# A four-layer graph network on one core: twelve stored pairs in place of ten, slots cleared by ScalarE, codes made behind takes

## What is computed

```python
def _rgcn_conv(x, src, dst, edge_type, edge_weight, W, root, bias):
    xj = x[src]
    m = jnp.zeros((xj.shape[0], W.shape[2]), dtype=x.dtype)
    for r in range(W.shape[0]):
        mask = (edge_type == r).astype(x.dtype)[:, None]
        m = m + mask * (xj @ W[r])
    m = m * edge_weight[:, None]
    out = jax.ops.segment_sum(m, dst, num_segments=x.shape[0])
    return out + x @ root + bias
...
h = jax.nn.relu(_rgcn_conv(x, src, dst, edge_type, ew, W1, root1, b1))
h = _rgcn_conv(h, src, dst, edge_type, ew, W2, root2, b2)
...
x = _layernorm(x + _L3_gnn_ref(...), axis=-1)
```

## Time and profile before

| | |
|---|---|
| median of 3 runs | 3843.97 us (3838.03 to 3846.60) |
| the profiled execution | 3840.92 us, span 3838.9 us |
| mean granted TensorE clock | 0.957 |
| TensorE / VectorE / ScalarE / POOL busy | 3455.1 / 2470.5 / 2042.3 / 2647.7 us |
| first late pass, first to last gather | 1990.6 to 2929.6 us |
| second late pass, first to last gather | 2946.3 to 3826.2 us |

### The profile page before, as it was taken

How to read it: one execution, slowest core, us unless ns; L and a number is a source line. 1 busy time by engine, 2 the same in 40 slices (tenths; PEclk the granted TensorE clock), 3 DMA queues, 4 the chain that set the end, 5 groups by cost and what they waited for, 6 DMA issues and landing times. The chain is left out here.

```text
span 3838.9 us, 70907 instructions
## 1 busy us (share of the span) xinstructions
PE 3455.1 (90%) x23412; PEld 2961.8 (77%) x23412; DVE 2470.5 (64%) x7952; ACT 2042.3 (53%) x4808; POOL 2647.7 (69%) x2736
## 2 busy tenths in 40 slices
PE   6999999999999999699978888888886899999995
PEld 5999888998887888588856666676665778888885
DVE  6999998998976555766666665666562354444431
ACT  4555555555546555556565555555555444544453
POOL 5777777777752666365547777777776777777776
PEclk8999999999999999799989999999997999999997
DMA  7666666666675666466634444444443444444453
GB/s 232 191 190 191 187 190 182 189 193 188 186 214 129 157 160 158 112 161 171 171 102 149 145 151 146 149 149 154 143 154 100 132 142 150 150 141 144 148 157 91
DMA packets 438499, 609.19 MB, mean 159 GB/s; under 512 B 266274, under 2 KB 310818, under 8 KB 437987
## 3 DMA queue, kind: packets, MB, share of 16 engines
q1 hardware_dynamic: 310162, 342.89, 28.6%
q0 software_dynamic: 100624, 234.79, 23.5%
q10 hardware_dynamic: 27330, 26.78, 2.3%
HBM read 451.89 MB, written 152.35 MB: 157 GB/s over the span
## 5 line engine op out<-in xcount | busy, mean ns | idle before, releaser
L660 POOL DMA_INDIRECT work<-table_rel,reli x1454 | 1378.2, 948 | 488.7 <-issue 435.6
L660 POOL DMA_INDIRECT work<-table_pre,srci x831 | 815.5, 981 | 263.2 <-issue 259.6
L2709 ACT ACTIVATE work<-iota,local 128x72 f32<-128x72 f32 x1456 | 376.4, 341 | 456.4 <-PE bank L1715 452.0
L1715 PEld LDWEIGHTS bank<-work 128*128 128x128 f32 x2912 | 392.6, 203 | 231.6 <-DMA work<-table_rel,reli 213.8
L1715 PE MATMUL bank<-work 128*128 128x72 f32 x2912 | 405.6, 285 | 163.6 <-DMA work<-table_rel,reli 162.9
L2714 ACT ACTIVATE work<-work,ew,src_both 128x72 f32<-128x72 f32 x1456 | 512.1, 434 | 6.1
L1416 PE MATMUL bank<-counts,piece_hi 128*128 128x468 f32 x1176 | 462.0, 393 | 17.2 <-issue 9.6
L1044 ACT ACTIVATE X<-bank 128x468 uint8<-128x468 f32 (+1 forms) x624 | 327.8, 544 | 280.9 <-PE bank L986 276.4
L947 PE MATMUL bank<-w_both,work 128*128 128x256 f32 x1664 | 433.7, 386 | 18.3 <-DVE work L881 9.8
L1416 PE MATMUL bank<-counts,piece_lo 128*128 128x468 f32 x1176 | 448.0, 381 | 0.0
L959 PE MATMUL bank<-work 128*128 128x64 f32 x3328 | 400.5, 274 | 3.7 <-DVE hist L828 2.9
(11 more groups left out here) (335 smaller groups left out, 6022.0 us busy)
## 6 DMA issues: line engine op xcount, KB each, us to landing
work<-ea_cols SPq DMA_DIRECT2D x208, 256.0 KB, 2.9
kept<-work SPq DMA_DIRECT2D x50, 720.0 KB
kept<-w_both SPq DMA_DIRECT2D x50, 720.0 KB
work<-kept SPq DMA_DIRECT2D x50, 720.0 KB
w_both<-kept SPq DMA_DIRECT2D x50, 720.0 KB
adj<-X SPq DMA_DIRECT2D x156, 225.0 KB
work<-adj SPq DMA_DIRECT2D x60, 585.0 KB
work<-table_rel,reli POOLq DMA_INDIRECT x1454
```

The source lines that it names most:

```text
L660: pool.indirect_dma_start(into[:, u, :], None, tables[p], bass.IndirectOffsetOnAxis(ap=idx_of(p)[:, t:t + 1].bitcast(U32), axis=0)).then_i ...
L1715: mm = pe.matmul(bank[4 + m % LATE_BANKS][:, 0:PAIR_WIN], late_gat[n % LATE][:, u, :], late_hot[:, n % LATE_HOTS, u * PAIR_WIN:(u + 1) * P ...
L2709: ins = act.activation(hot3[:, u, :], iota[:, 0:PAIR_WIN], ACT.Abs, bias=local[:, t:t + 1], scale=-1.0)
```

## The change

Lines are those of the changed file in the rows of order below, of the file before elsewhere.

- `PERIOD` goes from 10 to 8: twelve stored pairs, 8, 16, ... 96; 120 units in place of 100. Ten units fall on eight turns by `TURN`, so turns 1 and 5 of every eight use two units. Their columns are 37 wide in place of 36. The extra pairs of pass 4 stay six, from 19 on in steps of 16.
- The slot of the first unit of a turn is cleared by ScalarE (`clear_slot`), at the end of step h, for the unit that is used at turn h-1; VectorE waits for it. A second unit of a turn is still cleared by VectorE.
- VectorE makes the codes of unit k+2 behind the takes of unit k, one tile's low parts behind each of four codes (`tile_lo`, `extra_lo`), and loads a half's registers behind the half before.
- In pass 3 TensorE begins a turn that uses two units with the use of the first. In pass 4 the extra unit's use moves from the middle of the turn to a place ahead of the next fill's first half and of the pair's.
- Some small arrays move to other places.

```diff
-PERIOD = 10
+PERIOD = 8
-GW = 36
+GW = 37
-UNIT_AT = {PERIOD * (k // (2 * RANGES)) + k % (2 * RANGES): k for k in range(D_UNITS + 1)}
-BUILD_AT = {h - 1: k for h, k in UNIT_AT.items()}
+TURN = (0, 1, 1, 2, 3, 4, 5, 5, 6, 7)
+TURNS_OF = [PERIOD * (k // len(TURN)) + TURN[k % len(TURN)] for k in range(D_UNITS + 1)]
+USED_AT = {h: [k for k in range(D_UNITS + 1) if TURNS_OF[k] == h] for h in range(-1, PAIRS + 6)}
+CLEARED_AT = {h: ks[0] for h, ks in USED_AT.items() if ks and 2 <= ks[0] < D_UNITS}
-X_EVERY, X_FIRST, X_N = 15, 17, 6
+X_EVERY, X_FIRST, X_N = 16, 19, 6
...
@@ late_dve
-                if p == 3 and BUILD_AT.get(h, D_UNITS) < D_UNITS:
-                    unit_codes(dve, BUILD_AT[h])
-                take_at = BUILD_AT if p == 3 else UNIT_AT
-                if h - 1 in take_at:
-                    unit_take(dve, p, take_at[h - 1])
-                if p == 3 and BUILD_AT.get(h + 1, 1) % RANGES == 0 and BUILD_AT[h + 1] < D_UNITS:
-                    half_lo(dve, BUILD_AT[h + 1] // RANGES)
+                for k in USED_AT.get(h if p == 3 else h - 1, ()):
+                    unit_take(dve, p, k)
...
@@ unit_codes
             ins.then_inc(code_ready, 1)
+            if n % RANGES and n // RANGES + 1 < D_UNITS // RANGES:
+                tile_lo(dve, n // RANGES + 1, n % RANGES - 1)
...
@@ unit_take
                 put_unit(dve, k)
+                if k + 2 < D_UNITS:
+                    unit_codes(dve, k + 2)
+                if (k + 1) % RANGES == 0 and k + 1 < D_UNITS:
+                    d_places[:] = load_within(dve, PAIRS + (k + 1) // RANGES * U + 1)
@@ put_unit
-            if k % RANGES == 0:
-                d_places[:] = load_within(dve, PAIRS + k // RANGES * U + 1)
-            if k >= 2:
-                dve.wait_ge(a_used, USES_BEFORE + k - 1)
-                dve.wait_ge(a_stored[k % 2], KEPT_BEFORE + k // 2 * 16)
-            done(dve, dve.memset(late_a[k % 2][:, :, :, TW:], 0.0))
+            if k in CLEARED_AT.values():
+                dve.wait_ge(high_or_clear, CLEARS_BEFORE + list(CLEARED_AT.values()).index(k) + 1)
+            else:
+                if k >= 2:
+                    dve.wait_ge(a_used, USES_BEFORE + k - 1)
+                    dve.wait_ge(a_stored[k % 2], KEPT_BEFORE + k // 2 * 16)
+                done(dve, dve.memset(late_a[k % 2][:, :, :, TW:], 0.0))
...
@@ late_pe
+                second_half = new[-1] if len(new) > 1 or len(used) > 1 and new else D_UNITS
+                if p == 3 and len(used) > 1:
+                    unit_use(pe, p, used.pop(0))
+                if new:
+                    unit_fill(pe, new[0], 0)
+                if p == 4 and h - 1 in X_AT:
+                    extra_use(pe, X_AT[h - 1])
                 if p == 4 and h in X_AT:
                     extra_fill(pe, X_AT[h], 0)
...
                 node(pe, h)
-                if build < D_UNITS:
-                    unit_fill(pe, build, 2)
-                if p == 4 and h - 1 in X_AT:
-                    extra_use(pe, X_AT[h - 1])
+                if len(used) > 1:
+                    unit_use(pe, p, used.pop(0))
+                if new and new[0] != second_half:
+                    unit_fill(pe, new[0], 2)
+                if len(new) > 1:
+                    unit_use(pe, p, used.pop(0))
+                    unit_fill(pe, new[1], 0)
                 if p == 4 and h in X_AT:
                     extra_fill(pe, X_AT[h], 2)
                 if not built:
                     pair_half(pe, p, h, 1)
-                if unit < D_UNITS:
-                    unit_use(pe, p, unit)
+                if second_half < D_UNITS:
+                    unit_fill(pe, second_half, 2)
+                for k in used:
+                    unit_use(pe, p, k)
...
+        def clear_slot(act, k):
+            act.wait_ge(a_used, USES_BEFORE + k - 1)
+            act.wait_ge(a_stored[k % 2], KEPT_BEFORE + k // 2 * 16)
+            act.activation(late_a[k % 2][:, :, :, TW:], zeros_b[:, 0:GW - TW].unsqueeze(1).unsqueeze(1)
+                           .broadcast_to([P, RHI, RELS, GW - TW]), ACT.Copy).then_inc(high_or_clear, 1)
@@ late_act
                 node(h - LATE_HOTS)
+                if p == 3 and h - 1 in CLEARED_AT:
+                    clear_slot(act, CLEARED_AT[h - 1])
```

More of the change, by code:

```diff
@@ L261, in gnn @@
         d_lo = b2b_row[:, 0:D_COLS]
-        d_w = [b1a_row[:, i * D_COLS:(i + 1) * D_COLS] for i in range(PIECES)]
+        d_w = [b1a_row[:, i * D_COLS:(i + 1) * D_COLS] for i in range(PIECES - 1)]
         d_sum = more[:, 0:2 * GC].rearrange("p (o c) -> p o c", o=2)
@@ L276, in gnn @@
         x_codes, *x_w = (src_hi[:, x_at + i * X_COLS:x_at + (i + 1) * X_COLS] for i in range(1 + PIECES))
-        x_lo = b2b_row[:, D_COLS:D_COLS + X_COLS]
+        x_lo = count[:, D_COLS + X_COLS:D_COLS + 2 * X_COLS]
+        x_end = x_at + (1 + PIECES) * X_COLS
+        d_w.append(src_hi[:, x_end:x_end + D_COLS])
         staging_x = view(11280 + D_COLS, X_COLS).bitcast(I32)
@@ L1461, in late_dve @@
                 built_setup(dve, in_dense, d_tmp, d_first, d_lo, d_code, d_w)
-                half_lo(dve, 0)
+                for u in range(U):
+                    tile_lo(dve, 0, u)
                 dense_setup(dve)
             else:
-                extra_lo(dve, 0)
+                for u in range(U):
+                    extra_lo(dve, 0, u)
             places = {}
             if p == 3:
-                unit_codes(dve, BUILD_AT[-1])
+                d_places[:] = load_within(dve, PAIRS + 1)
+                for n in range(2):
+                    unit_codes(dve, n)
+            else:
+                x_places[:] = load_within(dve, PAIRS + D_COLS + 1)
             for h in range(PAIRS + LATE_LAG):
@@ L1549, in dense_setup, with tile_lo, extra_lo @@
             done(dve, dve.tensor_copy(places[:, :, 0:1], firsts[0:1, :, 0:1]))
[L1551 to L1565, removed]
+        def tile_lo(dve, half, u):
+            at = half * U + u
+            for i in range(PIECES):
+                dve.tensor_scalar(late_lo[:, half % 2, u * PIECES + i, :], iota_b[:, :], d_lo[:, at:at + 1],
+                                  d_w[i][:, at:at + 1], ALU.is_equal, ALU.mult)
+        def extra_lo(dve, half, u):
+            at = half * U + u
+            for i in range(PIECES):
+                dve.tensor_scalar(late_lo[:, half % 2, u * PIECES + i, :], iota_b[:, :], x_lo[:, at:at + 1],
+                                  x_w[i][:, at:at + 1], ALU.is_equal, ALU.mult)
         def unit_codes(dve, n):
@@ L1590, in extra_codes @@
             ins.then_inc(code_ready, 1)
+            if k % RANGES and k // RANGES + 1 < X_UNITS // RANGES:
+                extra_lo(dve, k // RANGES + 1, k % RANGES - 1)
         def extra_take(dve, k):
@@ L1605, in extra_take @@
                 put_tile(dve, x_a, u, x_places).then_inc(x_taken, 1)
+            if (k + 1) % RANGES == 0 and k + 1 < X_UNITS:
+                x_places[:] = load_within(dve, PAIRS + D_COLS + (k + 1) // RANGES * U + 1)
         def extra_sum(dve, k):
@@ L1610, in extra_sum, with uses, builds @@
                 dve.tensor_copy(x_sum[:, k // RANGES % 2, :], bank[X_BANK][:, 0:GC]).then_inc(x_summed, 1)
+        def uses(h):
+            return [k for k in USED_AT.get(h, ()) if k < D_UNITS]
+        def builds(h):
+            return uses(h + 1)
         def takes_before(p, k):
@@ L1662, in late_pe @@
             if p == 3:
-                unit_fill(pe, BUILD_AT[-1], 0)
-                unit_fill(pe, BUILD_AT[-1], 2)
+                unit_fill(pe, 0, 0)
+                unit_fill(pe, 0, 2)
             for h in range(PAIRS):
                 m = (p - 3) * PAIRS + h
-                unit = UNIT_AT.get(h, D_UNITS)
-                build = BUILD_AT.get(h, D_UNITS) if p == 3 else D_UNITS
+                used = uses(h)
+                new = builds(h) if p == 3 else []
                 if p == 3 and h == PAIRS - 1:
@@ L1678, in late_pe @@
                     if h in D_PAIRS:
-                        pe.wait_ge(a_taken, sums_taken(p, unit))
+                        pe.wait_ge(a_taken, sums_taken(p, USED_AT[h][0]))
                     else:
@@ L2013, in low @@
             def low(k):
-                dve.wait_ge(x_high, k + 1)
+                dve.wait_ge(high_or_clear, k + 1)
                 split_low(dve, k, rows[k])
@@ L2310, in pieces_low @@
             if k < CHUNKS:
-                dve.wait_ge(x_high, CHUNKS + k + 1)
+                dve.wait_ge(high_or_clear, CHUNKS + k + 1)
                 split_low(dve, k, X[:, k * CT:(k + 1) * CT, :])
@@ L2460, in late3_sp @@
             for h in range(-1, PAIRS + 4):
-                k = BUILD_AT.get(h, D_UNITS)
-                if k < D_UNITS:
+                for k in builds(h):
                     sp.wait_ge(a_taken, takes_before(3, k) + U)
@@ L2839, in late4_sp @@
             for h in range(PAIRS + 5):
-                if UNIT_AT.get(h, D_UNITS) + 2 < D_UNITS:
-                    load(UNIT_AT[h] + 2)
+                for k in uses(h):
```

(2 more changed lines are left out.)

12 lines of the change are left out of this document (4 added, 8 removed).

## The result

The changed kernel takes **3895.18 us** (median of 4 runs, 3892.89 to 3896.49), the kernel before 3845.28 us beside it; the ratio is 1.0128, 95% interval 1.0115 to 1.0141. It is slower by 50 us. The forecast was 3891.

What follows compares the result with a forecast made beforehand. POOL bounds the kernel before; after the change TensorE bounds the first late pass. First pass +67, second -20: +47 us on the profiled 3840.9, which is 3.1 below the median 3844.0, giving 3891 us; range 3806 to 3930.

Steps and rivals of the forecast that it cites:

- The stops: First late pass: TensorE stands for ScalarE's relu, delayed by the moved clear, 15 x 4.6 + 4 x 3.74 = 84 us.
- The first pass: First late pass, first to last gather: 922 us without waits for the relu, 1006 with them, 67 us longer than before.
- The second pass: Second late pass: POOL stays the bound at 860 us, TensorE needs some 835, so 20 us are gained.
- rival 4: Second late pass does not gain, TensorE at 885 us; +25, 3916 us; chance only within the forecast's 0.62.
- TensorE has become the bound: First late pass: with 862 us of own work TensorE, not POOL, sets the end, by 3 us, before waits for the relu.
- the stops change their cause: First late pass: nothing extra for the clock, since the 880 us before ran at 0.96 granted with 82 waits for gathers.
- 889 + 84 = 973: First late pass: TensorE through 96 turns at 15 + 862 + 12 = 889 us, plus 84 us of waits for the relu.
- rival 2: First late pass: each of 19 waits for the relu also costs some 1.8 us of clock; +34, 3925 us; chance 0.04.
- No wait, no gain: First late pass: codes behind takes cause no wait at the second fill and no gain against 12 us of waits kept.
- Rival 1: First late pass: no new wait at L2400 for the relu, pass ends at 922 us; -37, 3807 us; chance 0.24.

## Why the prediction was right

- **The stops.** I forecast 15 of 4.6 us where the pair is gathered and 4 of 3.7 where it is built, 84 us. Measured in the window: 15 of 4.5 and 4 of 3.65, 82.3 us. ScalarE's clear, priced at 1.06 us between two other sizes, took 1.09. Four experiments (the relu ahead, the clears back on VectorE, the clears alone, ten pairs) make this shown and not only argued.
- **The first pass.** 1006 us from first to last gather forecast, 1013.0 measured; +67 against +74.
- **The second pass.** 860 forecast, 857.8 measured. TensorE's waits for the take, 63.3 us before, are gone from its list, and rival 4 (they stay and take the gain) was tried: it costs 19 us of the kernel's time, 24 of the pass, where I had 25. Its words "240 + 60 products" should be 120 + 60, as in the sum.
- **Two terms were mis-sized against each other, and the sum hid it.** That the two errors nearly cancel was luck. I gave TensorE 862 us for its own work up to turn 96, and so had it as the bound by 3 us even without the stops ("**TensorE has become the bound**"). Between its first gathered matmul and the end of the last unit's product it worked 811.6 us with the relu ahead: 50 less, and it is not the bound there, since POOL ran at its own pace and TensorE waited 27.7 us for gathers. And I put nothing on the clock ("the stops change their cause"). With the stops the same work took 849.5 us, 38 more; from 2010 to 2890 the granted clock was 0.50 for 99 us, with the relu ahead for 37. So the changed kernel was through 965.5 us after the first gather, where the sum has 889 + 84 = 973. Behind turn 96 the sum has 33 us and the trace 47.5, with one more stop at the relu, 6.1 us at 2961.8, that I had not looked for. Why 862 was too much is not settled; it was scaled from a stage that ran at 0.96, which can be part of it.
- **The clock.** Each of the 19 stops has its own stretch at a granted clock of 0.50, 3.4 or 6.8 us long and 106 us in all, and between 2010 and 2960 there is none elsewhere: 0.53 granted over the 5 us behind the stop above, 1.00 on both sides. The earlier trace rows show the same behind one wait of 4.35 us. The 38 us are 2.0 us a stop, so rival 2 is right that the clock is paid on top, and its 1.8 us were about right; its time (3925) came out too long because the own work was 50 us too high. I weighed it against the wrong row, the average clock of the stage before, whose 82 waits for gathers are short, 2.7 us at most; the last section shows that short and long waits of one total are not alike.
- **VectorE's chain.** "No wait, no gain" for codes behind takes holds with ScalarE's clears as far as it was tried, with the relu ahead and POOL as the bound (2 us). It fails once VectorE clears (41 us): the codes then stand ahead of the clear in steps that begin late, and a sum copy that I had not placed in the chain makes some of them late.
- **Rival 1** (no new stop, 3807) did not come, but its time is what the kernel gives when the stop is taken out: 3801.

## What to carry to other kernels

An instruction that waits holds up all that stands behind it in its engine's order (here a clear of 1.09 us, behind whose wait TensorE stood 82.3 us): before moving even a 1 us clear to a half-idle engine, write down what stands behind it there and who needs that next. A stop on an engine that is not the bound cost nothing here and showed nothing in the time (83.1 us of stops, 3841.87 us against 3841.30), so a part that measured as harmless may cost all of its stops when a later part uses up the slack; test parts together with the one that moves the bound. When work is cut into a chain of producers, place every instruction of the consumer's queue that waits on the same event, small copies too. When a forecast comes true, compare its terms and not only its sum.

## What the runs showed of the hardware

In these runs TensorE's granted clock followed neither its busy time nor the total of its waits (figures below); what told the runs apart was the long stops. The cleanest pair is the kernel before with the relu ahead and with ScalarE's clears alone, both over 2010 to 2890, with the same work (4922 and 4926 records). The first has 120.0 us of waits in 119 pieces, none above 2.8 us, the second 120.5 us in 57 pieces, 20 of them of 3.5 to 4.5 us. The granted clock is 0.97 and 0.93:

```profile
2010.00:2890.00 880.00, 757.56 (x4922) 584.90 (x4920) 528.20 (x1292) 483.46 (x1543) 665.79 (x703) 0.97 0.45 149
...
2010.00:2890.00 880.00, 758.50 (x4926) 594.18 (x4926) 437.81 (x1196) 578.61 (x1633) 665.70 (x704) 0.93 0.45 149
```

The same shows with twelve pairs from 2010 to 2900. With the relu ahead there are 47 us of waits with a longest of 3.6, at 0.98; with the first product of a two-unit turn later, 61 us of waits in 65 pieces with a longest of 2.0, and the clock is higher:

```profile
2010.00:2900.00 890.00, 824.82 (x5551) 645.49 (x5551) 636.26 (x1523) 462.69 (x1464) 647.85 (x685) 1.00 0.49 166
```

A stop of 3.65 to 4.5 us in the changed kernel cost TensorE its length and, on the mean, 2.0 us more (38 us for 19). POOL's pace of indirect gathers was steady: where TensorE left the slots free, 735 of them took 917.3 to 917.8 us in four runs, one every 1.25 us. The same clear of 128x1040 took 1.09 us on ScalarE and 0.93 on VectorE.
